# A four-layer decoder: the looks of causal attention issued as pairs over four row groups, and two residual adds of the recurrence placed ahead of late rows

## The reference

```python
    def _L1_attn_ref(x, rms_weight, w_A, b_A, w_x, w_sidegate, w_output, w_o):
        residual = x
        norm = jnp.sqrt(jnp.mean(x * x, axis=-1, keepdims=True) + EPS)
        xn = x * (rms_weight / norm)
        A = jax.nn.sigmoid(jnp.einsum('bld,dn->bln', xn, w_A) + b_A)
        x_el = jnp.einsum('bld,dn->bln', xn, w_x)
        sidegate = jax.nn.sigmoid(jnp.einsum('bld,dn->bln', xn, w_output))
        gate = jax.nn.sigmoid(jnp.einsum('bld,dn->bln', xn, w_sidegate))
        h = _gated_scan(A, x_el * sidegate)
        y = gate * h
        return jnp.einsum('bln,nd->bld', y, w_o) + residual
...
    def _L3_attn_ref(x, Wq, bq, Wk, bk, Wv, bv, Wo, bo, gamma, beta):
        H = 16
        N_EMBD = 128
        B, T, _ = x.shape
        Dh = N_EMBD // H
        q = split_heads(x @ Wq + bq)
        k = split_heads(x @ Wk + bk)
        v = split_heads(x @ Wv + bv)
        att = jnp.einsum('bhtd,bhsd->bhts', q, k) * (1.0 / math.sqrt(Dh))
        causal = jnp.tril(jnp.ones((T, T), dtype=bool))
        att = jnp.where(causal[None, None], att, -jnp.inf)
        att = jax.nn.softmax(att, axis=-1)
        o = jnp.einsum('bhts,bhsd->bhtd', att, v)
        o = o.transpose(0, 2, 1, 3).reshape(B, T, N_EMBD)
        y = o @ Wo + bo
        return (y - mu) * jax.lax.rsqrt(var + EPS) * gamma + beta
...
    x = x + _L1_attn_ref(_layernorm(x, axis=-1), ...)
...
    x = x + _L3_attn_ref(_layernorm(x, axis=-1), ...)
```

## Time and profile before

| | |
|---|---|
| median of 3 runs | 1911.75 us (1900.8 to 1920.13) |
| profiled execution | 1909.3 us |
| its span | 1907.6 us, 1.7 us less than its own time |
| PE busy | 1676.2 us (88% of the span) |
| DVE busy | 1127.0 us (59%) |
| ACT busy | 971.7 us (51%) |
| POOL busy | 706.5 us (37%) |
| mean granted clock of TensorE | 0.95 |

### The profile page before, as it was taken

One profiled execution on the slowest core, in us unless ns is written; L12 is line 12 of the kernel. 1 busy time (PEld: TensorE's weight loads), 2 busy tenths in 40 slices (PEclk: granted clock), 3 DMA queues, 4 the chain that ended last, 5 costly groups with the idle time before them and its releaser, 6 DMA issues. The chain is left out here.

```text
span 1907.6 us, 50177 instructions
## 1 busy us (share of the span) xinstructions
PE 1676.2 (88%) x19970; PEld 1176.4 (62%) x19970; DVE 1127.0 (59%) x2410; ACT 971.7 (51%) x2317; POOL 706.5 (37%) x947
## 2 busy tenths in 40 slices
PE   6884899775799999999999878899999999999885
PEld 4332899343457888888888753567986655454332
DVE  4544445359657777787775443666657866554424
ACT  4552443448686666666665335234553353445552
POOL 1103311306356766676674301473016611223101
PEclk9997899896799999999999889899999999999998
DMA  7311786000041000000000040523643200000100
GB/s 296 134 42 54 202 241 207 27 1 1 1 164 30 24 15 25 14 18 21 14 26 14 25 199 1 130 76 112 169 131 86 62 3 1 2 2 1 41 1 24
DMA packets 75641, 125.69 MB, mean 66 GB/s; under 512 B 10696, under 2 KB 55120, under 8 KB 73776
## 3 DMA queue, kind: packets, MB, share of 16 engines
q1 hardware_dynamic: 67408, 106.69, 17.4%
q0 software_dynamic: 6912, 15.61, 2.7%
q10 hardware_dynamic: 1088, 0.13, 0.0%
HBM read 83.73 MB, written 38.67 MB: 64 GB/s over the span
## 5 line engine op out<-in xcount | busy, mean ns | idle before, releaser
L2902 DVE SCALAR_TENSOR_TENSOR big<-bank,pack,big 128x256 f32<-128x256 f32 (+2 forms) x384 | 182.9, 477 | 39.2 <-ACT mask L2791 23.5
L2790 ACT ACTIVATE big<-bank,pack 128x256 f32<-128x256 f32 x192 | 91.3, 476 | 129.1 <-PE bank L2598 124.7
L2123 ACT ACTIVATE pack<-bank 128x512 f32<-128x512 f32 x96 | 57.5, 599 | 160.2 <-PE bank L785 92.6
L3330 ACT ACTIVATE pt<-bank 128x1024 f32<-128x1024 f32 (+3 forms) x128 | 84.2, 704 | 105.8 <-PE bank L3176 105.6
L3360 DVE TENSOR_REDUCE part<-bank 128x8 f32<-128x1024 f32 (+1 forms) x80 | 95.6, 1220 | 68.3 <-PE bank L3157 68.2
L2508 POOL TENSOR_TENSOR big<-big,mask 128x256 f32<-128x256 f32 (+1 forms) x128 | 93.7, 732 | 89.0 <-DVE big L2902 55.0
L2585 PE MATMUL bank<-big 128*128 128x128 f32 x896 | 123.2, 284 | 1.5 <-issue 1.5
L2598 PE MATMUL bank<-y,pack 128*128 128x262 f32 (+1 forms) x384 | 120.8, 400 | 4.2 <-DVE big L2902 4.0
L783 PE MATMUL bank<-yh,wl 128*128 128x512 f32 x192 | 113.1, 589 | 12.0 <-issue 4.3
L1921 POOL DMA_INDIRECT pack<-results,where x64 | 67.3, 1051 | 150.5 <-PE bank L1992 136.4
L3099 POOL TENSOR_SCALAR_AFFINE_SELECT pt<-pt 128x256 f32<-128x256 f32 x128 | 53.8, 425 | 157.1 <-ACT pt L3330 156.7
(11 more groups left out here) (664 smaller groups left out, 4425.9 us busy)
## 6 DMA issues: line engine op xcount, KB each, us to landing
big<-in_experts SPq DMA_DIRECT2D x46, 516.0 KB
big<-in_big SPq DMA_DIRECT2D x1, 9216.0 KB, 26.0
gate<-big SPq DMA_DIRECT2D x32, 256.0 KB
z<-gate SPq DMA_DIRECT2D x16, 512.0 KB
pack<-routing SPq DMA_DIRECT2D x60, 128.0 KB
wide_sorted<-big SPq DMA_DIRECT2D x5, 1472.0 KB, 13.1
pack<-in_pack SPq DMA_DIRECT2D x1, 5910.5 KB, 21.2
pack<-wide_sorted SPq DMA_DIRECT2D x16, 256.0 KB, 3.2
```

Source lines behind the costliest of these rows:

```text
L2790: nc.scalar.activation(dst3(i), conv_in(i, 0), ACT.Copy, scale=weight(i, 3))
L2902: ins = nc.vector.scalar_tensor_tensor(out=d, in0=conv_in(i, back), scalar=weight(i, 3 - back), in1=d, op0=ALU.mult, op1=ALU.add)
L3330: nc.scalar.activation(dst, src, ACT.Exp, scale=-1.0).then_inc(s["weights"], 1)
```

## The change

In causal attention looks are issued two at a time. `look_pair` takes two consecutive looks, which are always the two halves `gp` 0 and 1 of the same keys and heads. It waits for both slots, and for each head issues the four matmuls of row groups 0, 1, 2 and 3 in turn. Where there is a mask, the identity matmuls of the first look come ahead of the wait for the second slot. In the units a pair always stands behind both weighs; which units have one is in `paired_units`. The reductions on DVE are the same, two behind each other. The number of matmuls and of reductions is unchanged.

In the recurrence `add(0)` and `add(1)` move ahead on DVE, `project_out(1)` ahead of `centre(2)` on PE, `variance(2)` ahead of `centre(3)`, and on ACT `invert(2)` ahead of `square(3)`.

```diff
@@ layers_3_and_4, PE
             def late_rows(b):
                 pe.wait_ge(s["kcopied"], 1)
                 late.join(pe, b)
+
+            def late_centre(b):
                 pe.wait_ge(late.s["done"], b + 1)
+                centre(b)
...
             project_in(1)
             project_out(0)
             late_rows(2)
-            centre(2)
             project_out(1)
+            late_centre(2)
             late_rows(3)
-            centre(3)
             variance(2)
+            late_centre(3)
             variance(3)
@@ layers_3_and_4, ACT
             square(2)
+            invert(2)
             square(3)
-            invert(2)
             invert(3)
@@ layers_3_and_4, DVE
             scan(1)
+            add(0)
             late.add(dve, 2)
             late.mix(dve, 3)
-            add(0)
+            add(1)
             late.add(dve, 3)
             normed(2)
-            add(1)
             normed(3)
@@ causal_attention
-    per_unit = [(0, 1, 2, 2) * 3 + (0, 1, 0, 0)] + [(0, 2, 2, 2) + (0, 1, 2, 2) * 2 + (0, 2, 2, 0)] * 2
...
+    paired_units = [(1, 2, 3, 6, 7, 10, 11, 14)] + [(1, 2, 3, 5, 6, 7, 9, 10, 11, 14)] * 2
+
+    def pair_in(u):
         b, m = divmod(u, UNITS)
-        return range(looks_by(b, m), looks_by(b, m + 1)) if b + 1 < B and m + 1 < UNITS else range(0)
+        if b + 1 < B and m in paired_units[b]:
+            return (b + 1) * LOOKS + (AHEAD if b == 0 else 0) + 2 * paired_units[b].index(m)
 
     ring = [("most", at) for at in range(LOOKS + AHEAD)]
     for u in range(B * UNITS):
-        more = list(looks_in(u))
-        ring += [("weights", 2 * u)] + [("most", at) for at in more[:-1]] + [("weights", 2 * u + 1)] + [("most", at) for at in more[-1:]]
+        ring += [("weights", 2 * u), ("weights", 2 * u + 1)]
+        if pair_in(u):
+            ring += [("most", pair_in(u)), ("most", pair_in(u) + 1)]
...
-            def look(at):
+            def look_pair(at):
                 b, n = divmod(at, LOOKS)
                 i, kind, key, w, js, gp = looks[n]
-                dst = both(place["most", at])
-                reuse(place["most", at])
...
+                dst = [both(place["most", at + d]) for d in range(2)]
+                for d in range(2):
+                    reuse(place["most", at + d])
...
+                    if kind == 0:
+                        for gl in range(2):
+                            nc.tensor.matmul(dst[d][:, sl(gl)], k.ident_bf, later4[:, :], start=True, stop=False, skip_group_check=True)
...
                 for c, j in enumerate(js):
-                    for gl in range(2):
-                        rows = sl(2 * gp + gl, 32)
-                        mm = nc.tensor.matmul(dst[:, gl * S + c * w:][:, 0:w], qj[b][rows, j * S + i * P:][:, 0:P], kd[b][rows, key:key + w],
-                                              start=kind != 0, stop=True, tile_position=(rows.start, 0), skip_group_check=True)
-                mm.then_inc(s["scores"], 1)
+                    for d in range(2):
+                        for gl in range(2):
+                            rows = sl(2 * d + gl, 32)
+                            mm = nc.tensor.matmul(dst[d][:, gl * S + c * w:][:, 0:w], qj[b][rows, j * S + i * P:][:, 0:P], kd[b][rows, key:key + w],
+                                                  start=kind != 0, stop=True, tile_position=(rows.start, 0), skip_group_check=True)
+                        if c == len(js) - 1:
+                            mm.then_inc(s["scores"], 1)
...
                     weigh(u, 0)
-                    for at in looks_in(u)[:-1]:
-                        look(at)
                     weigh(u, 1)
-                    for at in looks_in(u)[-1:]:
-                        look(at)
+                    if pair_in(u):
+                        look_pair(pair_in(u))
                 if 0 <= u - LAG < B * UNITS:
                     values(u - LAG)
```

More of the change, by code:

```diff
@@ L3037, in causal_attention @@
     LOOKS = len(looks)
-    per_unit = [(0, 1, 2, 2) * 3 + (0, 1, 0, 0)] + [(0, 2, 2, 2) + (0, 1, 2, 2) * 2 + (0, 2, 2, 0)] * 2
-    def looks_by(b, m):
-        return (b + 1) * LOOKS + (AHEAD if b == 0 else 0) + sum(per_unit[b][:m])
-    def looks_in(u):
+    paired_units = [(1, 2, 3, 6, 7, 10, 11, 14)] + [(1, 2, 3, 5, 6, 7, 9, 10, 11, 14)] * 2
+    def pair_in(u):
         b, m = divmod(u, UNITS)
-        return range(looks_by(b, m), looks_by(b, m + 1)) if b + 1 < B and m + 1 < UNITS else range(0)
+        if b + 1 < B and m in paired_units[b]:
+            return (b + 1) * LOOKS + (AHEAD if b == 0 else 0) + 2 * paired_units[b].index(m)
     ring = [("most", at) for at in range(LOOKS + AHEAD)]
     for u in range(B * UNITS):
-        more = list(looks_in(u))
-        ring += [("weights", 2 * u)] + [("most", at) for at in more[:-1]] + [("weights", 2 * u + 1)] + [("most", at) for at in more[-1:]]
+        ring += [("weights", 2 * u), ("weights", 2 * u + 1)]
+        if pair_in(u):
+            ring += [("most", pair_in(u)), ("most", pair_in(u) + 1)]
     place = {item: i for i, item in enumerate(ring)}
@@ L3139, in reuse @@
                     pe.wait_ge(s[name], n + 1)
-            def look(at):
+            def look_pair(at):
                 b, n = divmod(at, LOOKS)
                 i, kind, key, w, js, gp = looks[n]
-                dst = both(place["most", at])
-                reuse(place["most", at])
-                if at < 3:
-                    pe.wait_ge(s["y_ready"], (2, 2, B)[at])
-                    pe.wait_ge(s["ln"], (2, B, B)[at])
+                dst = [both(place["most", at + d]) for d in range(2)]
+                for d in range(2):
+                    reuse(place["most", at + d])
+                    if at + d < 3:
+                        pe.wait_ge(s["y_ready"], (2, 2, B)[at + d])
+                        pe.wait_ge(s["ln"], (2, B, B)[at + d])
+                    if kind == 0:
+                        for gl in range(2):
+                            nc.tensor.matmul(dst[d][:, sl(gl)], k.ident_bf, later4[:, :], start=True, stop=False, skip_group_check=True)
                 if n == 0:
                     pe.wait_ge(s["k_out"], b + 1)
-                if kind == 0:
-                    for gl in range(2):
-                        nc.tensor.matmul(dst[:, sl(gl)], k.ident_bf, later4[:, :], start=True, stop=False, skip_group_check=True)
                 for c, j in enumerate(js):
-                    for gl in range(2):
-                        rows = sl(2 * gp + gl, 32)
-                        mm = nc.tensor.matmul(dst[:, gl * S + c * w:][:, 0:w], qj[b][rows, j * S + i * P:][:, 0:P], kd[b][rows, key:key + w],
-                                              start=kind != 0, stop=True, tile_position=(rows.start, 0), skip_group_check=True)
-                mm.then_inc(s["scores"], 1)
+                    for d in range(2):
[5 more added lines that the diff above has]
+                            mm.then_inc(s["scores"], 1)
             def turn_most(b):
@@ L3217, in _ @@
             pe.wait_ge(s["consts"], 2)
-            for at in range(LOOKS):
-                look(at)
-                if at in (1, 7, 13):
+            for at in range(0, LOOKS, 2):
+                look_pair(at)
+                if at in (0, 6, 12):
                     project_qk(at // 6 + 1)
-                if at in (5, 11, 17):
+                if at in (4, 10, 16):
                     project_v(at // 6 + 1)
-            look(LOOKS)
+            look_pair(LOOKS)
             turn_most(0)
-            for at in range(LOOKS + 1, LOOKS + AHEAD):
-                look(at)
+            for at in range(LOOKS + 2, LOOKS + AHEAD, 2):
+                look_pair(at)
             for u in range(B * UNITS + LAG):
@@ L3421, in _ @@
                 v = u - LAG
-                for at in looks_in(u):
-                    most(at)
+                if pair_in(u):
+                    most(pair_in(u))
+                    most(pair_in(u) + 1)
                 if v >= 0 and v % 8 == 7 and v < B * UNITS:
```

## The result

| | before | after |
|---|---|---|
| median | 1906.28 us (4 runs, 1898.7 to 1920.13) | 1931.47 us (4 runs, 1926.33 to 1936.74) |
| ratio, 95% interval | | 1.014 (1.0102 to 1.0177): slower by some 25 us |
| profiled execution, span | 1909.3, 1907.6 | 1926.33, 1924.6 |
| recurrence, first to last matmul | 74.8 (339.5 to 414.3) | 69.0 (339.1 to 408.2) |
| causal attention, first to last matmul | 250.7 (1537.6 to 1788.3) | 279.1 (1527.7 to 1806.7) |

The recurrence came out 5.8 us shorter in the two profiles, causal attention 28.4 us longer (its matmuls alone span 250.7 us before, so the "some 243 us" given for that stage above is too small). Stages that the change does not touch differ by up to 8 us between the two profiles, which is why the two spans are only 17 us apart.

What follows compares the result with a forecast made beforehand. Causal attention was taken as bound by PE, the recurrence by a chain of waits. Attention +7.8 us and recurrence -4 us gave +3.8 on 1911.75, so 1915.5 us, range 1898 to 1931.

Steps and rivals of the forecast that it cites:

- A pair costs 1.10 us of PE: Attention: four row groups run at once, so a pair takes PE 1.09 us instead of two looks' 2.18.
- DVE's two reductions stand in each step between pairs: Attention: the next pair waits until both looks are reduced, 2.36 us; pair to pair 3.60 us unmasked, 4.57 masked.
- One behind the other, ready together: Attention's three-slot ring: both looks of a pair come ready together, so PE's saved work turns into waiting for DVE.
- Rival D: Attention: four row groups share one weight path, each chained pair grows by 0.9 us; 1945 us, chance 0.07.
- B: Rival: PE is the bound in attention and the ring never holds it; 1886 us, chance 0.12.
- C: Rival: attention as forecast, but the recurrence gives nothing as clock fall and stall move with it; 1919.5 us, chance 0.14.
- E: Rival: pairs shift work but chains come out even, attention 0 and recurrence -4; 1908 us, chance 0.15.
- where -4 was taken: Recurrence: the reordering brings inversion 3 forward from 378.20 to 373.4; -4 us taken, ends -5 and 0.
- The stretch ahead of the units: Attention before its units: DVE waits while PE writes both looks, 10.46 us a round; +1.2 us including the end.
- attention, +7.8 us with ends 4 and 12: Causal attention: +1.2 ahead and at the end, batch 0 +3.8, batches 1 and 2 +1.4 each.
- PE busy under 47 us: Sign in attention's batch 1: PE busy falls from 53.6 to under 47 us while the stretch stays 55 to 57.
- the overlap of neighbours that the prediction read from the earlier trace: Attention: work of other row groups starts before a look has ended, so pairs save less than 1.09 us each.

Runs made afterwards that it cites:

- e4: Changed kernel with extra identity matmuls filling PE's waits in units 0 to 3 of batch 0 and ahead of unit 14's pair; ratio 1.007 to the kernel before.
- e3: Changed kernel with the two looks of a pair in the same place but issued one after the other, on two row groups each; ratio 1.0051 to the kernel before.
- e6: Changed kernel with DVE's reduction of a look reading only the first half of the keys; ratio 0.9963 to the kernel before.
- e7: Kernel before with DVE's reduction of a look reading only the first half of the keys; ratio 0.9965 to the kernel before.
- e1: Kernel before with only the reordering of the recurrence; ratio 0.9968 to the kernel before.
- e2: Kernel before with only the paired looks in causal attention; ratio 1.0159 to the kernel before.
- e5: Changed kernel with ACT's two activations of invert_sums behind unit 14 instead of unit 13; ratio 1.0112 to the kernel before.
- e8: Changed kernel with sums behind unit 14, identity matmuls added in batch 0's first four units and two ahead of every pair; ratio 1.0059 to the kernel before.
- e10: Kernel before with recurrence reordered, order weigh, look, weigh, look in pair units, first look and second weigh issued in turns; ratio 1.0042 to the kernel before.

## Why the prediction was wrong

The forecast was 1915.5 us, +3.8 over the median before; measured is 1931.47, +25 over the median of 1906.28 that the kernel before had in the same comparison. The direction was right and the size was not.

**Right by its own steps.** A pair costs 1.10 us of PE, not 2. DVE's two reductions stand in each step between pairs (3.62 us measured), PE waits for them (21.3 us in all, where 15 to 25 was forecast), and the four-group turn gains nothing. The first four units of batch 1 take 14.71 us at full clock (e4), where 14.7 was forecast. "One behind the other, ready together" was the mechanism; e3, e6 and e7 bear it out. Rival D fell with the 1.10 us, B with the 3.62 us from pair to pair and batches of 57 to 61 us, C and E with e1 and e2. The recurrence gave -5.8 in the two profiles, some -6 by e1's ratio and -4.8 as the mean over all profiles, where -4 was taken. That the two profiles gave more than the far end of -5 is partly luck: ACT's 3.51 us of unexplained waiting fell into the profile before. The stretch ahead of the units proves nothing either way: it took 52.0 us before and 53.8 after, but 54.4 in e1 with the old looks and 52.1 in e2 with the pairs.

**The term that was mis-sized: attention, +7.8 us with ends 4 and 12; it measured +28.4.** Two steps failed.

The first is that every duration of PE was taken at full clock, as it stood in the trace of before, where PE hardly idled. I weighed the clock in the recurrence and forgot it in attention, where I had just forecast 15 to 25 us of new waits. In the profile after, the clock is at half for 44 us between 1527.7 and 1806.7, where it was for 3.4 before; e2, with the same attention code, has 41. The sign that I had named, "PE busy under 47 us", failed mostly by that: it was 52.28. At full clock it would have been 48.3, as an estimate (12.88 in e4's first four units of batch 1, 12.83, 13.09 and 9.49 in the three stretches above), against 52.95 for the same batch before. So ten pairs save 4.7 us of PE work, 0.47 each and not 1.09: the overlap of neighbours that the prediction read from the earlier trace rows was there, and had taken more than half of the gain already. (That matmuls start in order would not have ruled it out, as the prediction took it: the 32 records of a pair are issued in turn and still run at once.) From e5 to e8, which differ by the filling, the batches lose 3.2, 2.0 and 2.0 us. Batch 3, without looks, and the end of the stage lasted 45.9 us after and 44.3 before, the same work, with 3.4 us of half clock in it; but e1, with the old looks, also took 45.9, so these 1.6 us cannot be put down to the pairs.

The second is a queue that I did not look at. The pair in unit 14 waits for the newest exponential, and I took ACT as free for it; two activations of `invert_sums` stood ahead. My 11.5 us for units 12 to 15 was 13.15 at full clock (batch 2, 1747.72 to 1760.87). I had found that moving the looks behind the second weigh adds a wait for ACT, but not named what was queued on ACT ahead. From the changed kernel to e5 the batches lose 2.6, 1.3 and 1.2 us and the end of the stage 2.1, clock included (0.5 without it: 43.8 in e5, 44.3 in e4).

How much each step makes, for a batch like 1 or 2 (units 0 to 3, 4 to 7, 8 to 11, 12 to 15):

| | us | sum |
|---|---|---|
| forecast | 14.7, 14.7, 15.0, 11.5 | 55.9 |
| changed kernel at full clock | 14.71 (e4), 14.92, 15.32, 13.15 | 58.1 |
| the last four with the sums later (e5) | 12.37 | 57.3 |
| measured | 16.08, 14.92, 15.32, 14.93 (batch 1) | 61.25 |

The forecast's own four parts add up to 55.9 and not to the 56.1 that it wrote, so its attention term should have read +7.4. Of the 5.3 us that a batch missed, 3.1 are the clock, 0.8 the two activations ahead on ACT, and 1.4 are steps at full clock that I had too short, above all the last four units (12.37 for 11.5); why these are longer I have not taken apart. Batch 0 took 57.0 us for a forecast of 48.7: e8, with filling and the sums later, takes 51.2, so 5.8 us are clock and ACT's queue, and 2.5 are short steps, 1.4 of them in the first four units (15.9 for 14.5). The three batches make 18.6 us of the 20.6 by which the term was off. The other 2 lie ahead of the units and at the end of the stage, where kernels with equal code differ by as much.

The filling is not free: at full clock units 0 to 3 take 14.87 us in e8 and 14.71 in e4, units 8 to 11 15.77 in e8 and 15.32 in the changed kernel. So e8 understates a little what the clock costs.

## What to carry to other kernels

Saving work on an engine that alternates with a second one over a short ring of buffers paid here only where the order kept one item in flight between them. Two items that must be free together and come ready together turned the second engine's time into part of every step (3.6 us, of which 2.4 are DVE), and e10 has such waits for two items with different readers. When a forecast adds waits to PE, price every matmul near them at half clock too. And when an item is moved to wait for the newest result, read the whole queue of the engine that makes it.

## What the runs showed of the hardware

Less PE work made PE's matmuls slower. The clock fell to 0.50 after waits of no more than 0.43, 0.54 and 0.64 us between bursts (e4, at 1670.8), and e8, with more matmuls in the same places, kept it at 1.00 and was faster than e5 by 0.5% in ratio. In the changed kernel's batches it also fell behind longer waits, of 2.15 us (ahead of the first weigh, at 1583.7) and of 1.73 us (in unit 14, at 1631 and 1693).

The four row groups of the array work side by side. 32 records of 128 columns take 1.10 us on four groups, and 16 records take 1.09 us on two. The same holds for 16 records of 256 columns: 1.07 us in a pair (1605.80 to 1606.88), in line with the prediction's step of about 0.11 us for each 128 columns in a group and some 0.2 us of start-up.
